# Attention and a top-4 expert layer on one core: slot tables from three engines, ranks and bias rows at other places, and twelve transposes of the identity ahead of the gathered rows

## What is computed

```python
def reference(x, ctx, router_w, router_b, gate_up, gate_up_b, down, down_b):
    # x, ctx: (4, 256, 256); 16 heads of 16
    x = x + mha(layernorm(x), ctx, ctx)      # causal, softmax
    t = layernorm(x).reshape(1024, 256)
    logits = t @ router_w.T + router_b       # 16 experts
    top_val, top_idx = top_k(logits, 4)
    scores = zeros.at[row, top_idx].set(softmax(top_val))
    gu = einsum('th,ehd->etd', t, gate_up) + gate_up_b
    gate, up = minimum(gu[..., ::2], 7), clip(gu[..., 1::2], -7, 7)
    h = (up + 1) * gate * sigmoid(1.702 * gate)
    out = einsum('etd,edh->eth', h, down) + down_b
    return x + (out * scores.T[:, :, None]).sum(0)
```

## Time and profile before

| what | us |
|---|---|
| median of 3 runs | 308.63 |
| the three runs | 306.86, 308.63, 311.17 |
| profiled execution | 307.52 |
| its span | 305.8 |
| TensorE busy | 271.9 (89%) |
| GpSimd busy | 192.6 (63%) |
| VectorE busy | 181.6 (59%) |
| ScalarE busy | 122.8 (40%) |

### The profile page before, as it was taken

How to read it: one execution, slowest core, us unless ns; L and a number is a source line. 1 busy time by engine, 2 the same in 40 slices (tenths; PEclk the granted TensorE clock), 3 DMA queues, 4 the chain that set the end, 5 groups by cost and what they waited for, 6 DMA issues and landing times.

```text
span 305.8 us, 5699 instructions
## 1 busy us (share of the span) xinstructions
PE 271.9 (89%) x1566; PEld 180.8 (59%) x1566; DVE 181.6 (59%) x484; ACT 122.8 (40%) x289; POOL 192.6 (63%) x232
## 2 busy tenths in 40 slices
PE   7688897698998754699999999999999999999895
PEld 7555565365575544446565665666666656656584
DVE  3997757967967898125444544544554656556433
ACT  3425565264465310243443443443453434334310
POOL 6992825624436989632877778777878777766400
PEclk9999999999995965769999999999999999999999
DMA  7606220010269396283554554554555555445574
GB/s 245 240 3 181 58 92 0 3 55 0 64 180 354 105 325 222 72 224 128 83 93 75 75 90 87 76 92 83 76 86 89 74 87 79 85 71 82 94 224 137
DMA packets 26877, 34.33 MB, mean 112 GB/s; under 512 B 2800, under 2 KB 21200, under 8 KB 26848
## 3 DMA queue, kind: packets, MB, share of 16 engines
q0 software_dynamic: 8592, 12.32, 25.7%
q1 hardware_dynamic: 17984, 21.39, 21.4%
q10 hardware_dynamic: 272, 0.26, 0.2%
HBM read 23.46 MB, written 10.43 MB: 111 GB/s over the span
## 4 chain that ended last, share of the span: by engine, by line
PE 67%; DVE 16%; DMA 5%; issue 5%; POOL 3%; ACT 1%; SPq 1%; ACTq 0%; POOLq 0%; DVEq 0%
PE ps L1495 24%; PE ps L1514 11%; DVE neg_max L877 6%; PE ps L1491 4%; PE ps L1311 4%; PE ps L1473 4%; PE ps L1235 3%; PE ps L1528 3%; PE ps L1504 3%; PE ps L1254 3%; DMA ctx_tok<-y_rows,slot_tok 2%; DMA br_sb<-n_L_ffn_router_bias_dram 2%; PE ps L1260 2%; PE ps L1287 2%; DVE x_tok L909 1%
## 5 line engine op out<-in xcount | busy, mean ns | idle before, releaser
L1495 PE MATMUL ps<-w_all,q_norm 128*128 x188 | 90.3, 603 | 0.0
L658 POOL DMA_INDIRECT acc_rows<-x_tok,slot_tok x44 | 70.1, 1593 | 31.1 <-ACT x_tok L813 25.7
L1159 DVE TENSOR_SCALAR v_aug<-ps 128x256 f32<-128x256 f32 x47 | 19.9, 424 | 71.2 <-PE ps L1495 51.3
L651 POOL DMA_INDIRECT ctx_tok<-y_rows,slot_tok x47 | 46.6, 991 | 16.2 <-issue 14.0
L1514 PEld LDWEIGHTS ps<-w_all,o_t 128*128 128x128 f32 x188 | 35.6, 190 | 25.7 <-issue 23.2
L797 ACT ACTIVATE v_aug<-v_aug 128x256 f32<-128x256 f32 x47 | 19.6, 417 | 76.1 <-DVE v_aug L1159 76.1
L1495 PEld LDWEIGHTS ps<-w_all,q_norm 128*128 128x128 f32 x188 | 35.1, 193 | 24.9 <-issue 23.0
L1514 PE MATMUL ps<-w_all,o_t 128*128 x188 | 48.3, 380 | 1.4 <-ACT o_t L802 1.4
L561 POOL TENSOR_SCALAR_AFFINE_SELECT w_all<-w_all 128x256 f32<-128x256 f32 (+1 forms) x48 | 23.4, 505 | 37.2 <-ACT w_all L711 36.4
L877 DVE TENSOR_REDUCE neg_max<-ps 128x2 f32<-128x512 f32 (+1 forms) x48 | 30.5, 683 | 7.6 <-PE ps L1260 7.6
L711 ACT ACTIVATE w_all<-ps 128x512 f32<-128x512 f32 x48 | 25.5, 599 | 23.2 <-PE ps L1287 23.2
(11 more groups left out here) (156 smaller groups left out, 382.4 us busy)
## 6 DMA issues: line engine op xcount, KB each, us to landing
w_all<-_L_ffn_gate_up_proj_dram SPq DMA_DIRECT2D x16, 512.0 KB, 5.4
w_all<-in_L_ffn_down_proj_dram SPq DMA_DIRECT2D x16, 256.0 KB, 5.8
acc_rows<-x_tok SPq DMA_DIRECT2D x8, 256.0 KB, 8.5
x_tok<-in_x_dram SPq DMA_DIRECT2D x4, 256.0 KB, 4.3
y_ext<-acc_rows SPq DMA_DIRECT2D x4, 256.0 KB, 4.3
vblk_hot<-acc_rows SPq DMA_DIRECT2D x4, 256.0 KB, 3.9
out_dram<-y_ext SPq DMA_DIRECT2D x4, 256.0 KB, 2.2
ctx_tok<-in_ctx_dram SPq DMA_DIRECT2D x3, 256.0 KB, 4.9
```

What stands on the lines that cost most here:

```text
L651: pool.indirect_dma_start(out=xg[:, i % XG, :], out_offset=None, in_=y_dram[:, :], in_offset=bass.IndirectOffsetOnAxis(ap=slot_tok[:, i:i ...
L658: pool.indirect_dma_start(out=acc[i % 2][:, :], out_offset=bass.IndirectOffsetOnAxis(ap=slot_tok[:, i:i + 1], axis=0), in_=o_sb[:, i % 3, ...
L1495: mm = pe.matmul(o, x_t[:, i % 3, k, :], w_all[:, bass.ds(e, 1), k * 2 * F:(k + 1) * 2 * F].rearrange("p a n -> p (a n)"), start=False, st ...
```

## The change

The tables are made by three engines. ScalarE gets a way of its own, `spread`: for four groups, four activations of |value - column| into `low_dist` (which reuses the attention mask's memory), and one Relu over all four, which leaves 1 (low) or the token number (high) where the distance is 0. It makes the lows of groups 0 to 7 and 16 to 19 and the highs of 16 to 23 and 28 to 31. VectorE keeps the lows of 8 to 15, 20 to 23 and 24 to 31 and the highs of 24 to 27; GpSimd the highs of 0 to 15.

Moved: in the order of the last batch R0 goes ahead of V1 and V2, and L1 ahead of V3; `router_scores(0)` on VectorE goes from behind the top of part 1 to behind `places(0)`. On TensorE `down_rows(1)` goes ahead of the last tokens' transposes, `scores_t(1)` ahead of the logits of part 2 and `down_rows(2)` ahead of its ranks. On ScalarE `b_rows(1)`, `scores_turned(1)` and `b_rows(2)` come earlier; on SP `b_rows_out(2)` goes ahead of `y_rows(2)`. `gate_up(0)` waits for three b_rows instead of four.

Added: four transposes of the identity ahead of `down_rows(3)` and eight behind it, into the bank of the first x turn. No DMA is added or removed.

```diff
-    ("V", b, (0,)), ("Y", 2, (0,)), ("S", b, (5,)), ("V", b, (1, 2)), ("R", 0, (0,)),
-    ("V", b, (3,)), ("L", 1, (0,)), ("V", b, (4, 5, 6, 7)), ("R", 1, (0,)), ("O", b, (0, 1))]
+    ("V", b, (0,)), ("Y", 2, (0,)), ("S", b, (5,)), ("R", 0, (0,)),
+    ("V", b, (1, 2)), ("L", 1, (0,)), ("V", b, (3,)), ("V", b, (4, 5, 6, 7)), ("R", 1, (0,)), ("O", b, (0, 1))]
...
             y_rows(1)
+            b_rows_out(2)
             y_rows(2)
-            b_rows_out(2)
...
             hot_blocks(0, pairs_of(0)[8:])
             counted(2)
-            hot_blocks(2, pairs_of(2)[:4])
...
+            def spread(table, source, part, first, scale, peak):
+                act.wait_ge(vblk_ready, part + 1)
+                act.wait_ge(low_ready, part + 1)
+                fwait(act, act_hot_ready, chunks[0])
+                for c in range(4):
+                    act.activation(low_dist[:, c, :], iota_h[:, :], ACT.Abs, bias=source[:, first + c:first + c + 1],
+                                   scale=-1.0).then_inc(dist_ready, 1)
+                chunks[0] += 1
+                act.wait_ge(dist_ready, 4 * chunks[0])
+                act.activation(table[:, first:first + 4, :], low_dist[:, :, :], ACT.Relu, bias=peak,
+                               scale=scale).then_inc(act_hot_ready, 1)
...
             top_exp(1)
+            act.wait_ge(work_full, slot_of[("X", B - 1, 11)] + 1)
+            spread_lows(0, 0)
             scores_turned(0)
+            spread_lows(0, 4)
             b_rows(0)
+            b_rows(1)
             tokens_high(B - 1)
-            b_rows(1)
+            scores_turned(1)
+            spread_highs(1, 16)
+            spread_highs(1, 20)
             top_exp(2)
+            spread_lows(1, 16)
+            spread_highs(2, 28)
+            b_rows(2)
             act.wait_ge(slots_full, 1)
             act.activation(slots_t[:, :], ps[:, 2, 0:P], ACT.Copy).then_inc(slots_t_ready, 1)
-            scores_turned(1)
             scores_turned(2)
-            b_rows(2)
             b_rows(3)
...
-                    if b == 1:
-                        router_scores(0)
                 elif kind == "R":
                     places(b)
+                    if b == 0:
+                        router_scores(0)
             router_scores(1)
             tokens(B - 1)
-            hot_lows(0)
+            hot_lows(0, pairs_of(0)[8:16])
             tokens_low(B - 1)
-            hot_highs(1, pairs_of(1))
-            hot_lows(1)
+            hot_lows(1, pairs_of(1)[4:8])
             router_logit(2)
             router_top(2)
             places(2)
-            hot_lows(2)
-            hot_highs(2, pairs_of(2)[4:])
+            hot_lows(2, pairs_of(2))
+            hot_highs(2, pairs_of(2)[0:4])
...
             def slots(part):
-                pe.wait_ge(vblk_hot_ready, PARTS[part][1] * TOP_K)
+                if part == 0:
+                    pe.wait_ge(vblk_hot_ready, NT // 2 * TOP_K)
+                pe.wait_ge(act_hot_ready, (2, 5, 6)[part])
                 pe.wait_ge(low_hot_ready, part + 1)
+                if part == len(PARTS) - 1:
+                    pe.wait_ge(late_high_ready, 4)
...
             scores_t(0)
             down_rows(0)
+            down_rows(1)
             tokens_t(B - 1)
-            down_rows(1)
+            scores_t(1)
             router_logits(2)
+            down_rows(2)
             ranks(2)
             counts()
             slots(0)
...
             block_slots()
-            scores_t(1)
             scores_t(2)
-            down_rows(2)
+            for _ in range(COVER // 2):
+                pe.transpose(ps[:, 2, 0:P], ident[:, :], ident[:, :])
             down_rows(3)
+            for _ in range(COVER):
+                pe.transpose(ps[:, 2, 0:P], ident[:, :], ident[:, :])
...
                 if i < 2:
-                    pe.wait_ge(b_rows_ready, B)
+                    pe.wait_ge(b_rows_ready, B - 1 + i)
```

More of the change, by code:

```diff
@@ L38 @@
 WARM_UP = 36
+COVER = 8
 def xattn_moe(nc, x, ctx_in, w_router, b_router, w_gu, b_gu, w_dn, b_dn, score_dram, out):
@@ L237, in xattn_moe @@
         low_ready = sem("low_ready")
+        dist_ready = sem("dist_ready")
+        act_hot_ready = sem("act_hot_ready")
         low_hot_ready = sem("low_hot_ready")
+        late_high_ready = sem("late_high_ready")
         live_ready = sem("live_ready")
@@ L772, in b_rows, with spread_lows, spread_highs @@
                                ACT.Copy).then_inc(b_rows_ready, 1)
+            chunks = [0]
+            def spread(table, source, part, first, scale, peak):
[9 more added lines that the diff above has]
+                               scale=scale).then_inc(act_hot_ready, 1)
+            def spread_lows(part, first):
+                spread(low_hot, low_f, part, first, -1.0, one_f[:, :])
+            def spread_highs(part, first):
+                spread(vblk_hot, vblk_f, part, first, -2.0 * T, tok_id[:, first // TOP_K:first // TOP_K + 1])
             top_exp(1)
+            act.wait_ge(work_full, slot_of[("X", B - 1, 11)] + 1)
+            spread_lows(0, 0)
             scores_turned(0)
+            spread_lows(0, 4)
             b_rows(0)
+            b_rows(1)
             tokens_high(B - 1)
-            b_rows(1)
+            scores_turned(1)
+            spread_highs(1, 16)
+            spread_highs(1, 20)
             top_exp(2)
+            spread_lows(1, 16)
+            spread_highs(2, 28)
+            b_rows(2)
             act.wait_ge(slots_full, 1)
             act.activation(slots_t[:, :], ps[:, 2, 0:P], ACT.Copy).then_inc(slots_t_ready, 1)
-            scores_turned(1)
             scores_turned(2)
-            b_rows(2)
             b_rows(3)
@@ L1038, in places, with hot_lows @@
                 dve.tensor_copy(low_f[:, tk], low_i[:, tk]).then_inc(low_ready, 1)
-            def hot_lows(part):
+            def hot_lows(part, pairs):
                 dve.wait_ge(low_ready, part + 1)
@@ L1044, in hot_lows @@
                     dve.wait_ge(work_full, slot_of[("T", B - 1, 7)] + 1)
-                pairs = pairs_of(part)
                 n = len(pairs)
@@ L1056, in hot_highs @@
                                       tok_id[:, j // TOP_K:j // TOP_K + 1], ALU.is_equal, ALU.mult
-                                      ).then_inc(vblk_hot_ready, 1)
+                                      ).then_inc(late_high_ready, 1)
             def live_blocks():
```

## The result

The changed kernel takes 311.93 us (median of 13 executions, 308.46 to 316.56) beside 310.03 (13 executions, 305.7 to 314.41) for the kernel before. The ratio is 1.0088, 95% interval 1.005 to 1.0125: a little slower, where 4.6 us less was forecast. The profiled execution has a span of 310.2 us beside 305.8.

What follows compares the result with a forecast made beforehand. The chain of waits up to the first gate/up matmul, then TensorE, was taken as the bound: gather 2.7, down_rows 0.8 and clock 1.1 sum to 4.6 us off the median 308.63, giving 304.0; range 301.5 to 307.5.

Steps and rivals of the forecast that it cites:

- Earlier turns: Last attention batch: moving R0, L1 and part 0's scores gains 0 to 1.05 us, 0.7 taken, despite V4's wait.
- R3: Rival, 6%: y_rows(2) held behind b_rows_out(2) on the SP queue, gather 4.0 us later; 2.1 us slower, 310.7.
- VectorE's way to the logits: Tables of part 2: first logits instruction at 113.5 instead of 115.70, 2.2 us earlier; live blocks at 120.1.
- GpSimd: Tables: its last four highs, 4.28 us, go; part 0's sixteen end near 116.4, last slot matmuls start at 120.15.
- ScalarE: Tables: six chunks of four Abs and one Relu, 2.0 us each, hidden below the live blocks by 0.35 us.
- R1: Rival, 14%: ScalarE becomes the bound with chunks of 2.3 to 2.5 us, gather 1.2 us earlier; 305.5.
- y_rows(2): Before the first gather: its landing at 123.1, not slot_tok, releases the gather at 123.4, 2.7 us earlier.
- The first turns: Ahead of the first gate/up matmul: twelve transposes hide in the wait; one down_rows less gains 0.8 us.
- The clock: First gate/up block: eight transposes before x's turns raise TensorE's clock sooner, 1.1 us gained.
- R4: Rival, 12%: little arrives; GpSimd's highs held longer, or V4's wait and a late clock rise; 0.5 to 2 us, 307.4.

Runs made afterwards that it cites:

- e9: Changed kernel with only L1 back behind V3, R0 and router_scores(0) still moved; ratio to the kernel before 0.994 (0.986 to 1.001).
- e10: Changed kernel with only R0 back behind V2, L1 still ahead of V3; ratio to the kernel before 1.002 (0.996 to 1.008).
- e6: Changed kernel with old last-batch order, y_rows(2) first, early router_scores(2), and b_rows_out(3) held until the second gathered block lands; ratio to before 0.994.
- e7: Changed kernel with old last-batch order, y_rows(2) first, early router_scores(2), and 15 more identity transposes in TensorE's waits; ratio to before 0.988.
- e12: e7 with the changed kernel's early R0 and router_scores(0), L1 behind V3; ratio to the kernel before 0.985 (0.979 to 0.990).
- e13: Changed kernel with four identity transposes in TensorE's wait in front of V4; ratio to the kernel before 1.005 (0.997 to 1.012).

## Why the prediction was wrong

**Earlier turns: the step that failed.** It said "Against it, V4 ... has to wait for ScalarE's copy `o_t`, 0.60 us", and took a gain of 0.7. The mechanism was seen and its direct price nearly right (0.80 measured). What was left out is what comes with it: it priced V3 to O from the trace before, where TensorE ran them at 2.4 GHz, as if the clock came with the instruction. In the changed kernel TensorE was at 1.2 GHz there, from 0.1 us ahead of var to 16.9 behind it (6.8 us in the trace before), and with the 0.80 of the wait the stretch took 3.35 us more, in place of 0.7 less. e9 and e10 show that of the moved turns it is L1 that costs; the wait of 0.80 is shown, and 3.4 us more at the lower level go with it. How much of the rest is L1's matmuls, and how much the moment at which the clock fell, stays open. Its bounds, 0 to 1.05 us gained, excluded a loss, and so did every other case but R3.

**VectorE's way to the logits: right.** Last y row to the first logits instruction 4.63 us (4.3 forecast, 5.76 before), to the live blocks 11.26 (10.9). The 0.4 missing are spread over many small instructions.

**GpSimd: right.** Its last eight highs took 7.82 us beside 9.83 before and 8.0 forecast, and nothing waited for them. **ScalarE: right.** The last chunk and what follows, in order of time:

```profile
123.10 1.28 ACT L785 ACTIVATE mask_diag<-iota_h,vblk_f 128x128 f16<-128x128 f16 x4 [0.54 <-DVE low_f L1071]
124.41 0.72 ACT L789 ACTIVATE vblk_hot<-mask_diag,tok_id 128x512 f16<-128x512 f16 x1
125.04 0.58 ACT L774 ACTIVATE x_tok<-ps 128x512 f32<-128x512 f32 x1
```

A chunk is 2.03 us, 2.0 forecast, and 1.97 by the Trainium skill's price (ScalarE: Activation LUTs, What ACT_TABLE_LOAD costs); the trace agrees. It ended 0.4 us before the live blocks (125.50), 0.35 forecast. So R1 was the right thing to fear and did not come. Four Abs took 1.28 us beside VectorE's 1.23 us two-input instruction (123.06) and 1.26 to 1.28 in the other chunks: the Trainium skill (SBUF — State Buffer, SBUF: two separate sides) says ScalarE never waits for the port that VectorE and GpSimd share, and the trace agrees.

**y_rows(2): named, mis-sized.** That the gather would wait for y_rows(2) and not for `slot_tok` is what happened; the landing took 2.25 us (2.2 forecast) and sharing the queue cost 0.1, so R3 is out. But the gather began 0.90 us after the landing, where I took 0.3, the step seen behind `slot_tok`. So live blocks to gather gained nothing, 4.00 beside 3.94, in place of 0.64. With the 0.4 above, 0.9 is left of the 2.0 us forecast between the last y row and the gather (16.19 before, 15.25 after).

**The first turns: wrong.** I gave 0.8 us for one `down_rows` less in front of x's turns. The second row block was what TensorE waited for, as I said, but it came later:

```profile
132.78 0.66 PE L1512 MATMUL ps<-ident,ctx_tok 128*128 128x128 f32 x2 [0.17 <-DMA ctx_tok<-y_rows,slot_tok]
134.39 0.69 PE L1512 MATMUL ps<-ident,ctx_tok 128*128 128x128 f32 x2 [0.95 <-DMA ctx_tok<-y_rows,slot_tok]
```

0.95 us idle and the second turn 4.9 us after the gather's issue, not 4.1. In the kernel before packets until 130.1 were read as the landing; the landing that a semaphore reports was not in that row. Of the 0.8 us nothing was there to be had: gather to gate/up 5.88 before, 5.8 to 6.5 in every variant. b_rows_out(3)'s issue, now 1.9 us after the gather's, may be part of it; e6 could not tell.

**The clock: wrong.** 1.1 us were forecast from the eight transposes. TensorE in stretches, kernel after:

```profile
130.00:132.00 2.00, 2.00 (x9) 0.50 0.23 59
...
134.00:136.00 2.00, 0.82 (x3) 0.50 0.45 131
136.00:138.00 2.00, 2.00 (x3) 0.50 0.44 130
...
140.00:142.00 2.00, 2.00 (x8) 1.00 1.00 360
```

It was busy with them at 130 to 132, then only 0.82 of 2.00 us in the wait for the second block, and the clock rose at 140, when the first gate/up matmuls were through, exactly as before. "The wait for the second gather leaves a hole" was in the text as a discount; here nothing of the 1.1 came. That the hole kept the clock down is argued, not shown: e7, with the same twelve transposes, had the higher level from 130.5, 6.2 us after its gather's issue, and e12 had not.

**R4** ("little of it arrives", with a clock that rises as late as before) comes nearest to what happened, at 12%: it names V4's wait too, but as what eats a gain (307.4), not as what makes a loss. A rival that ends slower through V4's wait and the clock in front of the tables was missing, and the range, 301.5 to 307.5, stood on a before of 308.63 where more executions give 310.03. Of the 7.9 us between 304.0 and 311.93, 1.4 are that.

## What to carry to other kernels

On TensorE a moved instruction takes its duration from the clock of its new neighbourhood: before moving a turn away from a wait that it covers, price the work behind it at both levels and put that into the range. When a wait is taken out of a chain, time the next releaser with its own delay: a GpSimd DMA began 0.9 us after another DMA's landing, 0.3 after a VectorE result. Where executions of one kernel spread by 3% with the granted clock, compare means over many with their clocks beside them, cut single traces at common events, and look in each for when the clock fell before calling a difference the edit's.

## What was not expected of the hardware

- The mean granted clock explains most of the spread between executions of one kernel: 2.3 us per 0.01, correlation -0.92 over the 13 executions of the changed kernel, -0.76 over 68 of the kernel before.
- Twelve transposes of the identity ahead of a wait of 0.95 us went with no earlier rise of the clock in the changed kernel; 26 in two waits of the kernel before went with a mean clock higher by 0.012.
- In the changed kernel TensorE was busy 4.00 of 4.00 us from 96.3, and its clock stayed at 0.50; in e9, with the same turns up to L1 and busy 4.00 of 4.00 from 96.5, it rose at 99.9. The two clocks had fallen 0.7 us apart against that work.
- A gather on GpSimd starts 0.9 us after the landing of the DMA it waits for (0.90 in the kernel after, 0.91 in e9, 0.90 in e13), and 0.3 us after VectorE's semaphore.
